# Relative attention with the weights stored from ACT's queue and new places for two products; mutual attention with the projection between the two turned weights

## What is computed

```python
gate = sigmoid(gate_in @ Wg.T + bg)
return gate * char2sub + (1 - gate) * sub2char
```

```python
attn1 = einsum('bhqd,bhkd->bhqk', rq, rk)
attn2 = einsum('bhqd,qkd->bhqk', rq, rel_k_table[clip(k - q, -32, 32) + 32])
attn = softmax((attn1 + attn2) / scale, axis=-1)
w1 = einsum('bhqk,bhkd->bhqd', attn, rv)
w2 = einsum('bhqk,qkd->bhqd', attn, rel_v_table[clip(k - q, -32, 32) + 32])
return (w1 + w2) @ Wo + bo
```

## Time and profile before

| what | value |
|---|---|
| time, median of 3 runs | 2785.98 us (2774.95 to 2787.11) |
| the profiled execution's own time | 2780.81 us |
| its span in the profile | 2779.1 us |
| PE, DVE, ACT, POOL busy | 85%, 55%, 44%, 22% of the span |
| granted TensorE clock, mean | 0.92 of full speed |
| mutual attention | about 195 to 535 us of the span |
| relative attention | about 1445 to 2350 us of the span |

### The profile page before, as it was taken

How to read it: one execution, slowest core, us unless ns; L and a number is a source line. 1 busy time by engine, 2 the same in 40 slices (tenths; PEclk the granted TensorE clock), 3 DMA queues, 4 the chain that set the end, 5 groups by cost and what they waited for, 6 DMA issues and landing times. The chain is left out here.

```text
span 2779.1 us, 53345 instructions
## 1 busy us (share of the span) xinstructions
PE 2356.9 (85%) x18240; PEld 1869.5 (67%) x18240; DVE 1537.0 (55%) x2929; ACT 1221.0 (44%) x2701; POOL 609.2 (22%) x682
## 2 busy tenths in 40 slices
PE   8989999788999999299957999999999997595047
PEld 5669999687999999277744666666666665352035
DVE  5866666583111111389954565665656664644865
ACT  2223332212334343166634555555555554436743
POOL 1101111165444443144421111111111210000000
PEclk9999999858999999699978999999999998697579
DMA  2223222173999999300025555555555552110211
GB/s 80 69 60 78 66 64 64 29 265 124 346 343 344 344 342 327 114 1 0 0 40 131 126 119 124 117 124 128 118 123 119 124 125 49 67 71 35 106 42 41
DMA packets 386450, 346.73 MB, mean 125 GB/s; under 512 B 70322, under 2 KB 364748, under 8 KB 384332
## 3 DMA queue, kind: packets, MB, share of 16 engines
q1 hardware_dynamic: 374092, 329.03, 41.6%
q0 software_dynamic: 12288, 16.79, 2.7%
HBM read 258.72 MB, written 87.05 MB: 124 GB/s over the span
## 5 line engine op out<-in xcount | busy, mean ns | idle before, releaser
L2099 ACT COPY rel_probT<-rel_ps_t 121x400 f32<-121x400 f32 x384 | 195.9, 510 | 258.0 <-PE rel_ps_t L2317 257.8
L2317 PE MATMUL rel_ps_t<-rel_ident,rel_prob 100*121 100x100 f32 x1536 | 248.1, 284 | 30.5 <-ACT rel_probT L2099 30.4
L2317 PEld LDWEIGHTS rel_ps_t<-rel_ident,rel_prob 100*121 100x121 f32 x1536 | 196.9, 186 | 105.0 <-ACT rel_probT L2099 75.3
L2111 ACT ACTIVATE rel_prob<-rel_ps_s,rel_nmx 100x361 f32<-100x361 f32 x512 | 264.1, 578 | 3.2 <-DVE rel_nmx L2200 3.2
L1266 PEld LDWEIGHTS moe_ps_h<-moe_xeT,moe_w 128*128 128x128 f32 x2048 | 240.2, 193 | 5.1 <-issue 1.9
L1266 PE MATMUL moe_ps_h<-moe_xeT,moe_w 128*128 128x128 f32 x2048 | 240.8, 276 | 1.3 <-DVE moe_xeT L1431 1.3
L2200 DVE TENSOR_REDUCE rel_nmx<-rel_ps_s 100x2 f32<-100x722 f32 x256 | 232.8, 909 | 8.8
L1266 PE MATMUL moe_ps_y<-moe_w,moe_hT 128*128 128x256 f32 x1024 | 231.4, 379 | 0.0
L2830 PE MATMUL ffd_ps_y<-ffn_w_dT,ffd_oq 128*100 128x256 f32 x384 | 86.1, 386 | 146.0 <-DVE ffd_oq L2775 140.4
L1266 PEld LDWEIGHTS moe_ps_y<-moe_w,moe_hT 128*128 128x128 f32 x1024 | 189.6, 190 | 23.2
L1257 ACT ACTIVATE moe_hT<-moe_ps_h,moe_b 128x128 f32<-128x128 f32 x512 | 142.4, 375 | 137.8 <-PE moe_ps_h L1266 137.4
(11 more groups left out here) (427 smaller groups left out, 4968.0 us busy)
## 6 DMA issues: line engine op xcount, KB each, us to landing
moe_w<-in_L_ffn_w SPq DMA_DIRECT2D x128, 1024.0 KB
rel_scores<-rel_r_ext SPq DMA_DIRECT2D x32, 818.8 KB
rel_r_key<-rel_scores SPq DMA_DIRECT2D x32, 818.8 KB
rel_weights<-rel_prob SPq DMA_DIRECT2D x128, 204.7 KB
rel_by_dist<-rel_weights SPq DMA_DIRECT2D x32, 400.0 KB
mut_ctx_nat<-in_ctx SPq DMA_DIRECT2D x32, 363.0 KB
mut_ctx_T<-in_ctxT SPq DMA_DIRECT2D x16, 722.0 KB
rel_ctx_T<-in_ctxT SPq DMA_DIRECT2D x32, 361.0 KB, 3.7
```

The costliest lines, as they stand in the source:

```text
L2099: nc.scalar.copy(probT[:, pg % 2, c], ps_pT).then_inc(s_t_sb, 1)
L2111: last = nc.scalar.activation(prob[:, t.parity, slot, :], ps_s[0:S, j, 0:L], ACT.Exp, bias=nmx[:, slot:slot + 1])
L2317: last = nc.tensor.transpose(ps_pT[:, j, :], prob[:, pt.parity, QUAD * pg + j, c * STEP:c * STEP + R], ident[0:S, 0:S])
```

## The change

Three things change.

- The stores of the weights to DRAM move from SP's queue to ACT's: in each group after the last copy of a turned piece. g3's weights are stored at the end of their own turn and not at the start of the next. The count of landed stores is kept in two semaphores by parity, and the store of g0 waits for the read by distance of two rows before. SP keeps the context load, the two reads and the store of distance scores.
- A place may hold several jobs. `d1` moves from after the last turned piece of g2 to right behind `d0`, before that piece. `out` moves from after the last piece of g3 to before it. The numbers of the jobs, and so their banks, stay. DVE's order of work is the same.
- In mutual attention the turned weights of the second batch row come after the next pair's projection.

```diff
--- before.py
+++ after.py
@@ -944,10 +944,10 @@
                     rows_turned(nxt)
                 if t.within(NP):
                     weights_turned(t, 0)
-                    weights_turned(t, 1)
                 if nxt.within(NP):
                     project(nxt)
                 if t.within(NP):
+                    weights_turned(t, 1)
                     sums_y(t)
                 if prev.within(NP):
                     pe.wait_ge(s_mixed, prev.i + 2)
@@ -1879,7 +1879,7 @@
         s_rout, s_rkey = sem("distances_in_dram"), [sem(f"distances_by_key{v}") for v in range(2)]
         s_s, s_add, s_neg, s_p = sem("scores"), sem("scores_added"), sem("maxima_negated"), sem("weights_ready")
         s_t, s_t_sb, s_pv, s_att = sem("weights_transposed"), sem("weightsT_stored"), sem("values_summed"), sem("sums_kept")
-        s_pout, s_pdist, s_far, s_far_sum = (sem("weights_in_dram"), sem("weights_by_distance"), sem("far_masked"),
+        s_pout, s_pdist, s_far, s_far_sum = ([sem(f"weights{v}_in_dram") for v in range(2)], sem("weights_by_distance"), sem("far_masked"),
                                              sem("far_summed"))
         s_stats, s_took = sem("stats_ready"), sem("waits_taken")
         block = ctx.enter_context(nc.Block())
@@ -1892,7 +1892,7 @@
         JOBS = [("after", "xT"), ("next", "k0"), ("after", "q"), ("next", "k1"), ("after", "r0"), ("next", "v0"),
                 ("after", "r1"), ("next", "v1"), ("last", "den"), ("last", "d0"), ("last", "d1"), ("last", "w2"),
                 ("next", "v2"), ("last", "out")]
-        PLACES = [0, 1, 2, 3, 4, 5, 6, None, 7, 8, 9, 10, 11, 12, None, 13]
+        PLACES = [[0], [1], [2], [3], [4], [5], [6], [], [7], [8], [9, 10], [], [11], [12], [13], []]
         NUMBER = {what: n for n, (_, what) in enumerate(JOBS)}
 
         def bank(what):
@@ -1925,14 +1925,13 @@
             n = NUMBER[what]
             eng.wait_ge(s_job_sb[n % 2], before(t, n, n % 2) + 1)
 
-        def job(t, place):
-
-            n = PLACES[place]
-            if n is None:
-                return None, None, None
-            who, what = JOBS[n]
-            b = t + AHEAD[who]
-            return (n, what, b) if b.within(B) else (None, None, None)
+        def jobs(t, place):
+
+            for n in PLACES[place]:
+                who, what = JOBS[n]
+                b = t + AHEAD[who]
+                if b.within(B):
+                    yield n, what, b
 
         def group(t, g):
 
@@ -1962,16 +1961,8 @@
                 sp.dma_start(p_rows[v, :, :, 0:REACH], zeros[:, :, 0:REACH]).then_inc(s_zero, 16)
             sp.wait_ge(s_zero, 64)
 
-            def store(b, g):
-
-                sp.wait_ge(s_p, GROUPS * b.i + (g + 2))
-                sp.dma_start(p_rows[b.parity, :, QUAD * g:QUAD * (g + 1), REACH:PW],
-                             prob[:, b.parity, QUAD * g:QUAD * (g + 1), 0:NEAR]).then_inc(s_pout, 16)
-
             def turn(t):
                 b, nxt, prev, after = t, t + 1, t + -1, t + 2
-                if prev.within(B):
-                    store(prev, GROUPS - 1)
                 if after.within(B):
 
                     if not isinstance(after.i, int) or after.i > 1:
@@ -1990,23 +1981,18 @@
                 if prev.within(B):
 
                     v = prev.parity
-                    sp.wait_ge(s_pout, 16 * GROUPS * prev.i + 16 * GROUPS)
+                    sp.wait_ge(s_pout[v], 16 * GROUPS * prev.half + 16 * GROUPS)
                     sp.sem_inc(s_took, 1)
                     if not isinstance(prev.i, int) or prev.i > 0:
                         wait_filled(sp, t + -1, "d1")
                     sp.dma_start(by_dist[:], bass.AP(p_rows.tensor, p_rows[v].offset,
                                                      [[NH * PW + 1, S], [PW, NH], [1, ND]])).then_inc(s_pdist, 16)
-                if b.within(B):
-                    store(b, 0)
                 if after.within(B):
                     if not isinstance(after.i, int) or after.i > 1:
                         sp.wait_ge(s_rkey[after.parity], 16 * after.half)
                         sp.sem_inc(s_took, 1)
                     sp.wait_ge(s_rpad, after.i + 1)
                     sp.dma_start(r_rows[after.parity, :, :, 0:NEAR], r_ext[:]).then_inc(s_rout, 16)
-                if b.within(B):
-                    store(b, 1)
-                    store(b, 2)
 
             turns(sp, turn, -2, 3, B - 3, B + 1)
 
@@ -2066,9 +2052,11 @@
             act.sem_inc(s_p, 1)
 
             def empty(t, place):
-                n, what, b = job(t, place)
-                if what not in ON_ACT:
-                    return
+                for n, what, b in jobs(t, place):
+                    if what in ON_ACT:
+                        take(t, n, what, b)
+
+            def take(t, n, what, b):
                 wait_filled(act, t, what)
                 if what == "xT":
                     nc.scalar.copy(xT[:], two(what)).then_inc(s_job_sb[n % 2], 1)
@@ -2104,7 +2092,7 @@
                 act.wait_ge(s_neg, PAIRS * t.i + (2 * g + k + 1))
                 if g == 0 and k == 0 and (not isinstance(t.i, int) or t.i > 1):
 
-                    act.wait_ge(s_pout, 16 * GROUPS * (t.i - 1))
+                    act.wait_ge(s_pout[t.parity], 16 * GROUPS * t.half)
                     act.wait_ge(s_far, t.i - 1)
                 for j in range(2 * k, 2 * k + 2):
                     slot = QUAD * g + j
@@ -2112,6 +2100,16 @@
                                                 bias=nmx[:, slot:slot + 1])
                 if k == 1:
                     last.then_inc(s_p, 1)
+
+            def store(b, g):
+                if not b.within(B):
+                    return
+                act.wait_ge(s_p, GROUPS * b.i + (g + 2))
+                if g == 0 and (not isinstance(b.i, int) or b.i > 1):
+
+                    act.wait_ge(s_pdist, 16 * (b.i - 1))
+                act.dma_start(p_rows[b.parity, :, QUAD * g:QUAD * (g + 1), REACH:PW],
+                              prob[:, b.parity, QUAD * g:QUAD * (g + 1), 0:NEAR]).then_inc(s_pout[b.parity], 16)
 
             def turn(t):
                 for g in range(GROUPS):
@@ -2124,6 +2122,7 @@
                     weights(t, g, 1)
                     empty(t, 4 * g + 2)
                     transposed(pt, pg, 2)
+                    store(t, g)
                     empty(t, 4 * g + 3)
 
             turns(act, turn, -2, 3, B - 3, B + 1)
@@ -2156,9 +2155,11 @@
             last.then_inc(s_ready, 1)
 
             def empty(t, place):
-                n, what, b = job(t, place)
-                if what is None or what in ON_ACT:
-                    return
+                for n, what, b in jobs(t, place):
+                    if what not in ON_ACT:
+                        take(t, n, what, b)
+
+            def take(t, n, what, b):
                 wait_filled(dve, t, what)
                 if what == "q":
                     if not isinstance(b.i, int) or b.i > 1:
@@ -2218,7 +2219,7 @@
                         dve.wait_ge(s_pv, GROUPS * prev.i + GROUPS)
                         nc.vector.tensor_copy(raw[:], ps_raw).then_inc(s_att, 1)
                     for k in range(4):
-                        if g == GROUPS - 1 and k == 3:
+                        if g == GROUPS - 1 and k == 2:
                             normalise(t + 3)
                         empty(t, 4 * g + k)
                     if g == 1 and prev.within(B):
@@ -2236,9 +2237,10 @@
             pe.wait_ge(s_ready, 1)
 
             def fill(t, place):
-                n, what, b = job(t, place)
-                if what is None:
-                    return
+                for n, what, b in jobs(t, place):
+                    put(t, n, what, b)
+
+            def put(t, n, what, b):
                 o = before(t, n, n % 2)
                 if not isinstance(o, int) or o > 0:
                     pe.wait_ge(s_job_sb[n % 2], o)
```

## The result

The changed kernel takes 2757.05 us (median of 5 runs, 2753.47 to 2757.62), the kernel before in the same set of runs 2779.37 us (5 runs, 2774.95 to 2787.11). The ratio is 0.992, 95% interval 0.9903 to 0.9936: faster by 0.8%. Forecast were 2780 us and a range that began at 2758. The profiled span went from 2779.1 to 2752.3 us. I split these 26.8 us by the same landmarks in both traces (`rel_far` are the weights beyond the reach, which POOL masks once a turn); 0.7 us lie behind the last of them.

The account below looks back on a forecast made before the run. TensorE's gaps were taken to bound relative attention: −0.06 − 0.15 + 0.3 = +0.09 us a turn, 31 turns, +2.8 us; mutual attention −1.6; so +1 us, forecast 2780 us, range 2758 to 2810.

Parts of the forecast that it names:

- ACT's stores held: End of g3 and g0: ACT's issues held behind SP's large transfers, delaying its copies; 0 to 0.5 us a turn, taken 0.3.
- earlier landing: Relative attention: distances land sooner with stores off SP, ending TensorE's two block waits; at most 0.31 us a turn, half taken.
- output ahead of the piece: End of g3: output product before the last turned piece lets the next scores start 0.56 us sooner a turn.
- distance block ahead of the piece: End of g2: the turned piece now stands behind the wait for DVE's reciprocal; 0.50 us more a turn.
- mutual attention: Sixteen turns: one TensorE gap closes and another opens before the sums; 0.1 us less a turn, 1.6 us in all.
- What ACT's stores cost: Forecast step on ACT's four DMA issues a turn in relative attention: g3's store held as on SP, 0.3 us a turn.
- Where the landing stays: Forecast step: a held g3 store lands later and delays the read by distance, giving back much of 2 us; gain 0.15 a turn.
- The landing's bound: Most an earlier landing of the distances could save: TensorE's two waits before the distance blocks, 0.31 us a turn.
- ACT is not held: Rival: ACT's stores cost 0.28 us in idle time and distances land sooner; 11 + 1.6 us less, 2768 us; chance 0.27.
- The two moves: Output product in g3 and second distance block in g2, relative attention: together 0.06 us less a turn.
- The distances land later: Rival: g0's store on ACT gets ahead of the read by distance, landing 1.06 us later a turn; 2810 us; chance 0.20.

Follow-up runs that it names:

- stores_only: Kernel before with only the four weight stores moved to ACT's queue; both products and mutual attention as before: 2771.86 us, ratio 0.9942.
- before_split: Kernel before with DVE's far sum in its own tile, a small copy waiting for the landing instead; stores on SP: 2768.13 us, ratio 0.9935.
- places_only: Kernel before with the output product and second distance block at their new places; stores on SP, projection at its old place: 2805.96 us, ratio 1.0082.
- mutual_only: Kernel before with only mutual attention's projection moved between the two turned weights: 2779.39 us, ratio 0.9981.
- no_d1: Changed kernel with the second distance block back behind the last turned piece of g2: 2752.33 us, ratio 0.9881.

## Why the prediction was wrong

The sum was +1 us and the forecast 2780; measured was a gain of 22 us. Point by point, in us a turn, with the stores on ACT's queue first and the moves made after that:

| step | on record | measured |
|---|---|---|
| ACT's stores held | +0.3 | 0 |
| earlier landing | −0.15, bound −0.31 | −0.46 |
| output ahead of the piece | −0.56 | −0.35 |
| distance block ahead of the piece | +0.50 | +0.33 |
| mutual attention | −0.10 | −0.16 |

- **The step that failed is "What ACT's stores cost".** I took rows 7, where SP's issue is held behind SP's own transfers, for what happens to ACT behind SP's transfers. The rows show a hold within one queue and nothing between two. The stores took 0.28 us in the changed kernel (127 of 128), and the one of g3 2.33 us when the read by key was put on the same queue. The rule that I had set beside the rows is from the Trainium skill, "Perfetto Trace Analysis", section "DMA Instruction — HWDGE (DVE, Sync)": one issuer at a time locks the descriptor generator. I stretched it to the time that a transfer is under way. The section has the generator freed once the descriptors are made, and the issue of the read by key was over 0.67 us before ACT's began (1814.64 + 0.29 to 1815.60), so it never said that ACT would be held. Nor do SP's rows of 1.83 and 4.53 us fit it, for they come behind issues that were over as well.
- **"Where the landing stays" named the right effect and gave it the wrong cause.** With no hold, g3's store still lands later: 7.4 us pass from it to the read by distance in stores_only, 3.8 before. Of the 2.3 us by which the read by key starts sooner only 0.8 are left at DVE's far sum (13.01 to 12.22 us after g0's scores), so "much of the 2 us" is given back as forecast; no run moves the read alone. But these 0.8 us were enough for all of the gain that a landing in time can bring: before_split, where DVE does not wait for it at all, has the same turns.
- **The landing's bound was too small.** I priced a late landing by TensorE's two waits of the blocks, 0.31 us a turn. That was right for what it names: 9.6 us in all. It left out that each of the two longest waits, 1.2 us, is followed by 3.4 us at the lower clock level, 1.56 us more: two turns of the profiled execution, 0.11 us on each of the 29. This makes 0.31 + 0.11 = 0.42 of the 0.46. The earlier trace rows had it in its 0.99, which I read as the 2.4 GHz level throughout. With half of the bound taken, this term was short by as much as the hold was over: 0.31 and 0.3 us a turn. The rival "ACT is not held", at 0.27, was the right mechanism, with 2768 us: 11 us short for want of the clock and of what is below.
- **The two moves** nearly cancel, −0.02 us a turn against the forecast −0.06, but for other sizes. For the block I set the full 0.50 us of the piece; when the landing is in time the old order had a gap of 0.29 that the new one lacks. For the output I had the next scores 0.05 us behind the exponentials; g0's two further waits make it 0.24 to 0.29. That the forecast for the pair is so near is luck.
- **"The distances land later"** did not come: TensorE waits nowhere for them. But its reasoning, that a late landing reaches the end of g2 in full once the block is ahead of the piece, agrees with what places_only shows, 1.0082.
- **Outside the 29 turns** the changed kernel is 12.8 us shorter, and the turns of mutual attention explain 2.6. Much of the rest differs as much between kernels that have the same code there. The arrival at the stage is as under mutual_only. The stage's first stretch took 56.9 us before and 51.6 after; it took 51.4 in before_split, with the stores on SP, 57.7 in stores_only and 56.2 in no_d1. The stretch after the turns took 85.0 us at a mean clock of 0.79 before, 81.8 at 0.84 after, and 82.7 at 0.84 in mutual_only, whose relative attention is that of the kernel before. So no run shows that these 5.2 and 3.2 us come from the change; with one trace of each kernel their cause stays open.

## What to carry to other kernels

When a DMA issue shows microseconds, look at what the same queue has outstanding, and ask what the engine of that queue has to do meanwhile. Do not put a large read behind small stores that wait for late work: with the stores on another queue the read started 2.3 us sooner in the turn, and though the stores then landed later, what depended on both came sooner. Judge a move of work on the bounding engine with the latest wait in mind: the same two moves changed 29 turns by −0.4 us where one transfer landed in time (765.03 against 765.46 in stores_only), and cost 0.8% of the kernel where it did not. Price a wait of the bounding engine with the clock after it, from the longest turns, not from a typical one.

## What the runs showed of the hardware

- A store issued by ACT beside SP's traffic takes 0.28 us, 0.96 us behind SP's read of 819 KB too. Behind the same read on ACT's own queue it takes 2.3 to 3.1 us.
- Waits that are already satisfied cost TensorE time when they stand behind the last one: two of them 0.19 to 0.24 us. Put ahead of it, they leave the scores 0.05 us behind the exponentials, as where there are none.
- Two waits of TensorE of 0.86 to 0.88 and 0.33 us, 1.3 us from start to start of what they delayed, are followed by 3.4 us at the lower level in both long turns of the kernel before. Waits of 0.61 and 0.44 to 0.49 us, one of each in most turns, are followed by none: the changed kernel's granted clock is 1.00 over 400 us.
